# A block band filled by transfers instead of copies, and small instructions folded, in an attention and a windowed six-layer stack

## Time and profile before

| | before |
|---|---|
| time, three runs | 5647.85, 5654.42, 5653.05 us (median 5653.05) |
| profiled execution, span | 5652.0 us (the page gives no other time of that execution) |
| busy, share of the span | PE 76%, PE weight loads 51%, DVE 80%, ACT 51%, POOL 48% |
| mean granted TensorE clock | 0.877 of full speed |
| DMA queue of SP | 24464 packets, 21.14 MB, 1.2% of 16 engines' span |

### The profile page before, as it was taken

The page is one execution under the profiler, slowest core; times in us unless marked ns, Lnnn a source line. Parts: engine busy times, 40 slices in busy tenths (PEclk is TensorE's granted clock), DMA queues, the critical chain, the costliest instruction groups (busy, mean ns, idle before and its releaser), DMA issues.

```text
span 5652.0 us, 101203 instructions
## 1 busy us (share of the span) xinstructions
PE 4315.0 (76%) x36832; PEld 2891.9 (51%) x36832; DVE 4512.7 (80%) x6295; ACT 2889.8 (51%) x5057; POOL 2714.7 (48%) x1600
## 2 busy tenths in 40 slices
PE   6777677777777777777777777777777777777776
PEld 4556454545455545555555455454545454555454
DVE  5666688888878888888888788888888888888886
ACT  3343355555555555555555555555555555555554
POOL 2111255554555555545555554555455545555553
PEclk8888888888888888988898888888888988888888
DMA  1000000000000000000000000000000000000000
GB/s 40 0 0 0 1 1 0 0 0 0 19 1 0 0 0 0 20 1 0 0 0 0 20 0 0 0 0 11 9 0 0 0 0 11 9 0 0 0 0 15
DMA packets 24564, 22.50 MB, mean 4 GB/s; under 512 B 8588, under 2 KB 21776, under 8 KB 23696
## 3 DMA queue, kind: packets, MB, share of 16 engines
q1 hardware_dynamic: 24464, 21.14, 1.2%
HBM read 19.04 MB, written 2.10 MB: 4 GB/s over the span
## 4 chain that ended last, share of the span: by engine, by line
DVE 50%; issue 20%; PE 16%; ACT 12%; DVEq 1%; POOL 0%; ACTq 0%; SPq 0%; DMA 0%; POOLq 0%
PE ps L1076 6%; DVE AQb L766 6%; DVE ss L746 4%; DVE area L766 4%; DVE mx L702 4%; DVE ss L744 4%; DVE lw L602 4%; PE ps L1060 3%; DVE area L704 3%; DVE area L755 3%; DVE area L781 2%; ACT G L466 2%; DVE area L720 2%; DVE ss L739 2%; PE ps L1071 2%
## 5 line engine op out<-in xcount | busy, mean ns | idle before, releaser
L338 POOL TENSOR_TENSOR area<-area,lsum 128x1024 f32<-128x1024 f32 x192 | 365.1, 1901 | 1175.7 <-DVE lsum L713 1175.7
L324 POOL TENSOR_TENSOR area<-area,tab 128x512 f32<-128x512 f32 x384 | 502.9, 1310 | 830.3 <-DVE area L755 830.3
L332 POOL TENSOR_TENSOR area<-area 128x1024 f32<-128x1024 f32 x192 | 528.6, 2773 | 326.9 <-DVE area L766 326.9
L991 PE MATMUL ps<-Wqkv,xsT 128*128 128x512 f32 x768 | 505.4, 794 | 208.3 <-DVE area L755 206.4
L1060 PE MATMUL ps<-ident,AQb 128*128 128x128 f32 x1536 | 308.5, 357 | 430.8 <-DVE xn L611 425.1
L325 POOL TENSOR_TENSOR area<-area,tab 128x512 f32<-128x512 f32 x384 | 605.6, 1577 | 0.0
L725 DVE COPY BD<-area 32x512 f32<-32x512 f32 x768 | 518.1, 675 | 31.6
L332 POOL TENSOR_TENSOR AQb<-AQb,area 128x1024 f32<-128x1024 f32 x192 | 533.7, 2780 | 16.2 <-DVE AQb L766 1.2
L1076 PEld LDWEIGHTS ps<-kbd,area 128*32 128x32 f32 x12288 | 433.3, 138 | 141.9 <-issue 122.9
L1076 PE MATMUL ps<-kbd,area 128*32 128x128 f32 x12288 | 504.8, 334 | 0.0
L1060 PEld LDWEIGHTS ps<-ident,AQb 128*128 128x128 f32 x1536 | 231.6, 179 | 533.2 <-DVE xn L611 447.6
(11 more groups left out here) (130 smaller groups left out, 9262.9 us busy)
## 6 DMA issues: line engine op xcount, KB each, us to landing
Wqkv<-ffn_Wqkv SPq DMA_DIRECT2D x6, 1536.0 KB, 6.5
...
qks<-ffn_q_scale SPq DMA_DIRECT2D x6, 32.0 KB, 3.4
```

The source lines that it names most:

```text
L324: pool.tensor_tensor(b4[:, :, 0:h], q4[:, :, h:DH], s4[:, :, 0:h], ALU.mult).then_inc((s_bq, s_bk)[j], 1)
L332: pool.tensor_tensor(AQ[t][:, col], AQ[t][:, col], BQ[:, col], ALU.add).then_inc(s_rot, 1)
L991: last = mm(PJ[0][:, b * 512:(b + 1) * 512], xt, Wqkv[:, b * 512:(b + 1) * 512], start=True, stop=True)
```

## The change

The diff does the following:

- **Band by DMA.** `PTr` and `BD` are laid out anew (`BD` [128, tile, window, head, 32 queries]), so that each block of the band is a plain 32 x 512 piece of 2 KB per partition. DVE's four and ACT's three or four copies per tile go; SP issues 7 (tile 0) or 8 (tile 1) transfers from SBUF to SBUF of 64 KB each. `values` waits for their semaphore `d_bd[t]`, and `turn` for the transfers that read `PTr` before. SP now walks the same steps as the other engines, with the loads of weights and scales put between the bands of the first two units of a layer.
- **Evictions.** `o_evac_a`, two copies of 128x512 out of PSUM, moves from DVE to ACT, to where `band_prev(n - 1, 1)` stood.
- **Newton step** of three instructions instead of four: the guess is taken smaller by a constant factor (a bias in ACT's Exp), and the last two instructions become one. The addition of eps goes into ACT's Ln as a bias and into a scalar_tensor_tensor.
- **The floor of the norms** (L746) gets an accumulator output that nobody reads.
- **Attention:** 1/sqrt(8) is put into the eviction of q, the reductions negate, and the tensor_scalar of L640 goes.

```diff
+GUESS = 0.5 ** (1.0 / 3.0)
+NEWTON = 1.5 / GUESS
...
-        PTr = area4[:, 1024:2048].rearrange("p (h b i) -> p h b i", h=HEADS, b=2)
+        PTr = area4[:, 1024:2048].rearrange("p (b h i) -> p b h i", h=HEADS, b=2)
         kbd = sb("kbd", [P, PAIRS, 2, WIN + SEQ])
-        BD = sb("BD", [P, TILES, HEADS, P])
+        BD = sb("BD", [P, TILES, NWIN, HEADS, WIN])
...
+        consts = sb("consts", [P, 2])
+        eps_c, guess_c = consts[:, 0:1], consts[:, 1:2]
+        junk = sb("junk", [P, 1])
...
+        N_BAND = (2 * NWIN - 1, 2 * NWIN)
+        d_bd = (d_bd0, d_bd1)
...
-            with sp.Fori(0, DEPTH - 1) as L:
-                sp.wait_ge(s_tab, 6 * L + 6)
-                load_scales(L + 1)
-                sp.wait_ge(s_pv, (L + 1) * SEQS * TILES)
-                load_qkv(L + 1)
-                sp.wait_ge(s_wo, (L + 1) * SEQS)
-                load_wo(L + 1)
-                sp.wait_ge(s_xne, (L + 1) * SEQS)
-                load_ln(L + 1)
-                sp.wait_ge(s_y, (L + 1) * SEQS)
-                load_ff(L + 1)
+
+            def band(n, t):
+
+                need_apart(sp, i_sp, s_T, 2 * n + t + 1)
+                need_apart(sp, i_sp, s_o, 4 * n + 2 * t - 2)
+                for w in range(NWIN):
+                    rows = slice(32 * w, 32 * w + 32)
+                    sp.dma_start(BD[rows, t, w, :, :], PTr[rows, 1, :, :]).then_inc(d_bd[t], 16)
+                    if w:
+                        sp.dma_start(BD[32 * w - 32:32 * w, t, w, :, :], PTr[rows, 0, :, :]).then_inc(d_bd[t], 16)
+                    elif t:
+                        sp.dma_start(BB[P - WIN:P, :, :], PTr[rows, 0, :, :]).then_inc(d_bd[t], 16)
+
+            def step(n, u, head, mid, ffn, layer):
+                fresh = head and not isinstance(n, int)
+                if fresh and isinstance(u, int) and u == 0:
+                    sp.wait_ge(s_tab, 6 * layer + 6)
+                    load_scales(layer + 1)
+                    sp.wait_ge(s_pv, (layer + 1) * SEQS * TILES)
+                    load_qkv(layer + 1)
+                if mid:
+                    band(n - 1, 1)
+                if fresh and isinstance(u, int) and u == 0:
+                    sp.wait_ge(s_wo, (layer + 1) * SEQS)
+                    load_wo(layer + 1)
+                    sp.wait_ge(s_xne, (layer + 1) * SEQS)
+                    load_ln(layer + 1)
+                if fresh and isinstance(u, int) and u == 1:
+                    sp.wait_ge(s_y, (layer + 1) * SEQS)
+                    load_ff(layer + 1)
+                if head:
+                    band(n, 0)
+
+            stack_steps(sp, step)
...
+            pool.memset(eps_c, EPS).then_inc(i_guess, 1)
+            pool.memset(guess_c, math.log(GUESS)).then_inc(i_guess, 1)
...
-                need(act, ready, 3 * n + 3)
-                act.activation(lw[:, 1, :], lw[:, 0, :], ACT.Ln).then_inc(lsem, 1)
+                need(act, ready, 2 * n + 2)
+                act.activation(lw[:, 1, :], mv[:, :, 1], ACT.Ln, bias=eps_c).then_inc(lsem, 1)
                 need(act, lsem, 2 * n + 1)
-                act.activation(lw[:, 2, :], lw[:, 1, :], ACT.Exp, scale=-0.5).then_inc(lsem, 1)
+                act.activation(lw[:, 2, :], lw[:, 1, :], ACT.Exp, bias=guess_c, scale=-0.5).then_inc(lsem, 1)
 
...
-                act.activation(AqT[:, :], TR[1][:, 0:SEQ], ACT.Copy).then_inc(a_qe, 1)
+                act.activation(AqT[:, :], TR[1][:, 0:SEQ], ACT.Copy, scale=A_SCALE).then_inc(a_qe, 1)
...
-                need(act, a_nm, 4 * n + g + 1)
+                need(act, a_mx, 4 * n + g + 1)
                 bank = 3 * (g % 2)
                 for h in range(4 * g, 4 * g + 4):
                     k = h - 4 * g
                     act.activation(E0[:, h, :], ps[:, bank, k * P:(k + 1) * P], ACT.Exp,
-                                   bias=nmx[:, 1, 0, h:h + 1], scale=A_SCALE)
+                                   bias=nmx[:, 0, h:h + 1])
                     last = act.activation(E1[:, h, :], ps[:, bank + 1 + k // 2, (k % 2) * SEQ:(k % 2 + 1) * SEQ], ACT.Exp,
-                                          bias=nmx[:, 1, 1, h:h + 1], scale=A_SCALE)
+                                          bias=nmx[:, 1, h:h + 1])
                 last.then_inc(a_e, 1)
 
...
-                act.activation(ss[:, 3, :], ss[:, 2, :], ACT.Exp, scale=-0.5).then_inc(s_iv, 1)
+                act.activation(ss[:, 3, :], ss[:, 2, :], ACT.Exp, bias=guess_c, scale=-0.5).then_inc(s_iv, 1)
...
-            def band_prev(n, t):
-
-                T = 2 * n + t
-                need(act, s_T, T + 1)
-                need(act, s_o, 2 * T - 2)
-                for w in range(NWIN):
-                    src = PTr[32 * w:32 * w + 32, :, 0, :]
-                    if w:
-                        last = act.activation(BD[32 * w - 32:32 * w, t, :, 32 * w:32 * w + 32], src, ACT.Copy)
-                    elif t:
-                        act.activation(BB[P - WIN:P, :, :], src, ACT.Copy)
-                last.then_inc(s_bdp, 1)
+            def o_evac_a(n):
+                for g in range(2):
+                    need(act, s_o, 4 * n + g + 1)
+                    need(act, s_wo, n)
+                    act.activation(oT[:, 0, 4 * g:4 * g + 4, :], SC[:, g, :].rearrange("p (c n) -> p c n", c=4),
+                                   ACT.Copy).then_inc(s_oe, 1)
 
             def o_evac_b(n):
                 for g in range(2):
                     need(act, s_o, 4 * n + g + 3)
-                    need(act, s_oe, 4 * n + 2)
                     act.activation(oT[:, 1, 4 * g:4 * g + 4, :], (TR[0], SC[:, 0, :])[g].rearrange("p (c n) -> p c n", c=4),
...
                 if head:
                     norm_guess(n, 0)
                 if mid:
-                    band_prev(n - 1, 1)
+                    o_evac_a(n - 1)
                 if head:
                     squares(n, 1)
                 if mid:
...
-                if head:
-                    band_prev(n, 0)
...
-                need_apart(dve, i_dve, chain, 3 * n + 1)
+                need_apart(dve, i_dve, chain, 2 * n + 1)
                 for t in range(TILES):
                     last = dve.bn_aggr(mv[:, t, :], stats[:, t, :])
                 last.then_inc(chain, 1)
-                dve.wait_ge(chain, 3 * n + 2)
-                dve.tensor_scalar(lw[:, 0, :], mv[:, :, 1], EPS, None, ALU.add).then_inc(chain, 1)
-
-            def newton(n, k, v, y0, t1, y1, chain):
-
-                dve.tensor_tensor(t1, y0, y0, ALU.mult).then_inc(chain, 1)
-                dve.wait_ge(chain, 4 * n + 1)
-                dve.tensor_tensor(t1, t1, v, ALU.mult).then_inc(chain, 1)
-                dve.wait_ge(chain, 4 * n + 2)
-                dve.tensor_scalar(t1, t1, -0.5, 1.5, ALU.mult, ALU.add).then_inc(chain, 1)
-                dve.wait_ge(chain, 4 * n + 3)
-                dve.tensor_tensor(y1, y0, t1, ALU.mult).then_inc(chain, 1)
-                dve.wait_ge(chain, 4 * n + 4)
 
             def normalised(n, dst, src, rsem, nsem, done):
+
                 need(dve, rsem, 2 * n + 2)
-                newton(n, TILES, lw[:, 0, :], lw[:, 2, :], lw[:, 3, :], lw[:, 4, :], nsem)
+                z, sq, y = lw[:, 2, :], lw[:, 3, :], lw[:, 4, :]
+                dve.tensor_tensor(sq, z, z, ALU.mult).then_inc(nsem, 1)
+                dve.wait_ge(nsem, 3 * n + 1)
+                dve.scalar_tensor_tensor(sq, mv[:, :, 1], EPS, sq, ALU.add, ALU.mult).then_inc(nsem, 1)
+                dve.wait_ge(nsem, 3 * n + 2)
+                dve.scalar_tensor_tensor(y, sq, NEWTON, z, ALU.subtract, ALU.mult, reverse0=True).then_inc(nsem, 1)
+                dve.wait_ge(nsem, 3 * n + 3)
...
-                dve.tensor_reduce(nmx[:, 0, 0, hs], ps[:, bank, :].rearrange("p (h k) -> p h k", h=4), AX.X, ALU.max)
-                dve.tensor_reduce(nmx[:, 0, 1, hs], ps[:, bank + 1:bank + 3, :].rearrange("p a (h k) -> p (a h) k", h=2),
-                                  AX.X, ALU.max).then_inc(a_mx, 1)
-                need(dve, a_mx, 4 * n + g + 1)
-                dve.tensor_scalar(nmx[:, 1, :, hs], nmx[:, 0, :, hs], -A_SCALE, None, ALU.mult).then_inc(a_nm, 1)
+                dve.tensor_reduce(nmx[:, 0, hs], ps[:, bank, :].rearrange("p (h k) -> p h k", h=4), AX.X, ALU.max, negate=True)
+                dve.tensor_reduce(nmx[:, 1, hs], ps[:, bank + 1:bank + 3, :].rearrange("p a (h k) -> p (a h) k", h=2),
+                                  AX.X, ALU.max, negate=True).then_inc(a_mx, 1)
...
-                need(dve, s_bdp, T)
-                dve.transpose(PTr[:, :, :, :].rearrange("p h b i -> p (h b i)"), Pr[:, t, :]).then_inc(s_T, 1)
-                need(dve, s_T, T + 1)
-                need(dve, s_o, 2 * T - 2)
-                for w in range(NWIN):
-                    rows = slice(32 * w, 32 * w + 32)
-                    last = dve.tensor_copy(BD[rows, t, :, rows], PTr[rows, :, 1, :])
-                last.then_inc(s_bdc, 1)
+                need(dve, d_bd[1 - t], 16 * N_BAND[1 - t] * (n + t))
```

(23 more changed lines are left out.)

21 lines of the change are left out of this document (11 added, 10 removed).

## The result

The changed kernel takes **5895.03 us** (median of 4 runs, 5888.59 to 5897.47), beside 5650.45 us (5647.78 to 5654.42) of the kernel before on the same chip: ratio **1.0431** [1.0416, 1.0445], 245 us slower. The forecast was 5410 us, faster, with a range up to 5610. The profiled execution took 5897.47 us, its span 5895.7 us, at a mean granted clock of 0.829 (before 0.877).

The account below looks back on a forecast made before the run. DVE was read as the bound (half the last chain, PE 16%), with PE not far behind. 5652 − 90 (attention) − 197 (units) + 44 (boundaries) = 5409, stated as 5410 us; forecast 5330 to 5500, range 5200 to 5610.

Parts of the forecast that it names:

- Attention: −90: Attention, all inputs: tensor_scalars held by POOL go, 81 us of ACT's wait plus 9 us of small pieces; bounds 60 and 100.
- The band there at 20.7: Unit's first half: tile 1's transfers landed 20.7 us after the softmax of tile 1; bounds 19.8 and 22.1.
- I take 1.5, since the low stretch is short: Values of tile 1 after PE's wait for the band: half clock costs 1.5 us, between 0 and 2.2.
- the output product at 3.84: Output product behind the values of tile 1: takes 3.84 us as before, ending at 29.2.
- Mask and scores take 2.6: Before the softmax of each tile: mask and scores take 2.6 us, the scores 1.95 of it.
- Second half: Softmax of tile 0 to softmax of tile 1: 12.7 us, set by ACT's queue, where it took 16.47 before.
- PE's gaps are now under 1 us: Unit's second half: PE's short gaps were the reason given for mask and scores of 2.6 us at full clock.
- Unit: 48.9: One unit of the stack: 36.2 + 12.7 = 48.9 us, 2.1 us less, −197 us over 94 full units.
- Boundaries: 8.8 each: Layer boundaries: scales load behind the band's transfers, nothing hides it; 5 × 8.8 = +44 us.
- What was taken at nothing: Stack unit: BD's new layout priced at nothing, and tile 0's band transfers taken as hidden.
- PE stays cold: Slower rival: half clock lasts through values and output product of the unit before; 52.3 us per unit, 5730 us, chance 0.12.
- a cold PE in the output product: Sign of being wrong: PE at the low clock in the output product behind tile 1's values.

Follow-up runs that it names:

- x7: The kernel before with the attention folds alone (scale in the query's eviction, negated maxima, no multiplication between): 5531.52 us, ratio to before 0.9781.
- x3: The changed kernel plus 14 mask products with unread results in PE's wait before the values of tile 1: 5482.83 us, ratio to before 0.9695.
- x1: The changed kernel with the band filled by DVE's and ACT's copies again instead of transfers: 5205.74 us, ratio to before 0.9206.
- x10: x8 with the next layer's scales asked for at the start of a layer: 5039.56 us, ratio to before 0.8919.
- x8: The changed kernel with tile 1's transfers shared between SP and ACT, and unread filler products at four waits of PE: 5060.26 us, ratio to before 0.8947.

## Why the prediction was wrong, step by step

- **Attention: −90, measured −124.** The wait that goes was priced rightly: idle time 179.6 − 94.8 = 85 us for 81. The rest, 39 us, is of the size that the clock explains, though nothing tests it apart: in the kernel before PE waited 5.31 us along with ACT, and twelve of its transpositions behind that took 3.01 us, 1.7 times as long apiece as those ahead of the wait (8 in 1.15), so 1.3 us more for each of 15 inputs. In 10 of the 16 inputs the values behind them took 3.64 and 1.93 us, in the other 6 and in all of x7 1.93 and 1.06. Together that is some 45 us.
- **The band there at 20.7, measured 21.4.** The issues lie 0.62 us apart and not 0.475, which is 1.0 more; PE starts 2.1 after the last issue and not 2.6, which is 0.5 less; 0.14 more until the first issue. This was bounded and is not what turned the sign, though the bounds were added up wrongly: landings of 2.0 and 3.9 us with starts 0.475 apart give 20.1 and 22.0, not 19.8 and 22.1. For the landing the Trainium skill (DMA: Bandwidth & Descriptors, Anatomy of one DMA), weighed in the prediction, was nearer than the rows of loads from HBM: its 2.15 us against 2.0 to 2.1 measured. That section fits transfers that GpSimd issues, and SP issues these, so the agreement is not a confirmation of it.
- **The step that failed: "I take 1.5, since the low stretch is short", and the output product at 3.84.** The clock was put in for the values alone, at 1.5 us, with 2.2 as the bound. It cost 2.6 us there (5.8 for 3.2) and 1.5 in the output product (5.38 for 3.84), together 4.1 us for 1.5. x3 shows that this is the clock and nothing else of the transfers: with the band as late as in the change, both are back at their old lengths in 65 of 71 units.
- **"Mask and scores take 2.6" at full clock, twice.** End of the output product to softmax of tile 0 was 8.5 us (3048.29 to 3056.75) for 7.0, since the scores took 3.51 for 1.95. Second half: 13.6 for 12.7, scores 3.59. The argument "PE's gaps are now under 1 us" was nearly true of the second half (the longest is 1.18 us, for xn) and did not keep the clock; ahead of the scores of tile 0 PE waits 2.02 us. Twice 1.6 us in the scores, not priced at all, of which 1.5 and 0.9 reached the unit.
- **Unit: 48.9, measured 54.6.** 0.7 + 2.7 + 1.5 + 0.9 = 5.8 us, all but the first of it in work of PE at half clock. From the other side, 4.7 of the 7.2 us by which the change's unit exceeds x1's come back in x3 (4.3 by the medians), where the scores are still slow in most units.
- **Boundaries: 8.8 each, measured 3.2 to 4.1** (x10 against x8, not in the changed kernel itself): the wait is there (POOL idles 12.9 us for the scales), but less than half of its price reaches the end. What covers the rest was not looked for.
- **What was taken at nothing: right.** The layout of BD costs nothing (the values in x3 take 1.10 and 0.65 us, as before), and tile 0's transfers are hidden (PE waits for nothing ahead of its values at 3022.67).
- **The rival that came true** is "PE stays cold", with a chance of 0.12. Its mechanism and its place are right; its price, 52.3 us per unit and 5730 us, lacks the two slow scores, and its "against" (PE recovered within some 4 us of work) was the error in short: in the changed kernel the 0.50 lasts through some 9 us of unbroken work. For this the rows of before had evidence that was set aside: half clock from the wait before xn to the next softmax, named in the rival itself. That wait was 4.52 us, and the wait of 1.99 us ahead of the scores of tile 0 cost nothing there, so the rows did not settle it, but they spoke for more than 0.12. One of the prediction's own signs of being wrong, a cold PE in the output product, is what came.
